# Self-attention of one core: six small moves in an order of work written out by hand

## The chip, the cores and the metric

One core of a Trainium2 chip runs the kernel. Times are device microseconds (us). The median of three runs before the change is 2024.88 us (2024.06 to 2028.83).

## The reference, cut to what matters

The input is x with 2 batches of 512 rows of 512 channels. Three blocks follow each other, each added to x:

```
x = x + cross_attention(layernorm(x), ctx)   # 8192 context rows, 16 heads
x = x + attention(layernorm(x))              # causal, 16 heads of 32
x = x + experts(layernorm(x))                # 16 experts, top 2
```

The self-attention, which the change touches, computes per head

```
q_amp, k_amp = softplus(x Wq_amp), softplus(x Wk_amp), each over its root mean square
q_phi, k_phi = pi * tanh(x Wq_phi), pi * tanh(x Wk_phi)
scores = q_amp cos(q_phi) . k_amp cos(k_phi) + q_amp sin(q_phi) . k_amp sin(k_phi)
out = softmax(scaled, causal scores) (x Wv) Wo
```

## The kernel before

The cross-attention fills the first 1550 us or so, the self-attention lies between 1572 and 1875 us, and the experts come after it. The change is in the self-attention alone.

The 1024 rows are eight tiles of 128. A tile t goes through two strands. The strand `ahead` makes its queries, keys and values: normalise (`xn`), transpose on TensorE (`turn`), copy out (`copy`, and `low` for the f16 remainder), the five projections (`p01`, `p23`, `p4`), the softplus (`abs`, `exp`, `ln`, and `relu` on ScalarE for tiles 2 and later, then `amp` on VectorE adds the two), `square`, `mean`, `mroot`, `norm` for the root mean square, `phase` (a table load, tanh, two sines and a table load back, all on ScalarE; the second sine waits for `tabs` on VectorE), `polar` (amplitude times sine and cosine, in two halves 0 and 1), and `qkT`/`qkC` (transposes and copies of queries and keys). The other strand attends: for each pair of heads p (64 pairs over the 8 tiles) `scoreT` on TensorE, `expT` on ScalarE, for two pairs together `cut` (mask and key sums) and then `valueT` on TensorE and `normT` on VectorE. `woT` is the output projection of a tile, `x3` adds it to x, `rT`, `rC`, `router`, `logit` and so on prepare the expert stage.

Round a of 8 pairs (pairs 8a to 8a+7) attends with tile a and prepares tile a+1; it has 16 slots, two per pair. `slot(a, k)` calls `ahead(a+1, k)`, then the steps for tile a-1 from a table (`carry`: slot number to steps), then the others. A pair p issues: `scoreT`, slot 2(p mod 8), `expT`, for odd pairs `normT` and `cut`, slot 2(p mod 8)+1, for even pairs `valueT`. `self_order` lists all of this once, and each engine runs through the same list and executes its own kinds in that order, strictly one after another. Nothing is reordered at run time, so a wait of one instruction holds all behind it on its engine.

Banks of the matmul accumulator are handed on by `empty(banks, semaphore, value)` and `fill(banks)`: the step that fills a bank waits for the semaphore that `empty` noted last. Banks 0 and 1 hold the `p01` result, which `abs`, `relu` (tiles 2 and later) or `amp` (tiles 0 and 1) read; `turn` and `router`/`colsum`/`cum` fill them next. Bank 3 is filled by `woT` after `phase` has read it.

Tiles 2 and later use f16 weights in two parts, a high part (`high`, two ScalarE copies per weight, line 1433) and the remainder (`rest`, two VectorE operations per weight, line 1774). Weights 0 and 1 are split before round 0, weights 2, 3 and 4 in round 0. `p23` of tile 2 (round 1, slots 0 and 2) needs the parts of weights 2 and 3, `p4` of tile 2 (round 1, slot 6) those of weight 4.

Lines: 1107 `turn`; 1121 and 1126 `p01`, `p23`, `p4` in f32 and f16; 1135 `qkT`; 1165 `scoreT`; 1180, 1184 and 1188 `valueT`; 1195 `woT`; 1497 `expT`; 1362 table load; 1761 `xn`; 1770 `amp`; 1784 `square`; 1788 and 1791 `mean`; 1802 `tabs`; 1808 `polar`; 1816 `qkC` of the keys; 1845 to 1856 `cut`; 1862 and 1866 `normT`; 1875 `x3`; 1890 `logit`; 1244 and 1250 `colsum` and `router`. `stats 1` (lines 1824, 1367, 1369, 1603 to 1609) makes the scale factors of rows 512 and up by a Newton step, and stands ahead of `expT 8`.

Of the kernel before, what the change touches and what calls it, by code (L numbers as in the profile page):

```python
# [23 lines left out]
HALVES = 2  # L24
# [366 lines left out]
def self_order(kept):  # L391
# [5 lines left out]
    out, emptied = [], {}  # L397

    def fill(banks):
        return tuple(emptied[b] for b in banks if b in emptied)  # L400

    def empty(banks, name, value):
        for b in banks:
            emptied[b] = (name, value)

    def p23(t, n):
        out.append(("p23", t, n, fill((2 + n // 2,)) if n % 2 == 0 else ()))

    def p01(t, n):
        out.append(("p01", t, n, fill((n // 2,)) if n % 2 == 0 else ()))  # L410

    def p4(t, n):
        out.append(("p4", t, n, fill((1,)) if n == 0 else ()))

    def turn(t):
        out.append(("turn", t, fill((0,))))
        empty((0,), "xTs", t + 1)

    def qkT(t, w, half):
        out.append(("qkT", t, w, half, fill((2 + half,))))  # L420
        empty((2 + half,), ("QT", "KT")[w], 2 * t + half + 1)

    up = (10, 11, 12, 14)

    def ahead(t, slot, begun=False):
        if slot < 4 and not begun:
            p23(t, slot)
        if slot < 3:
            out.append((("abs", "exp", "ln")[slot], t))
        if slot == (3 if begun else 2) and t >= HALVES:  # L430
            out.append(("relu", t))
        if slot == 3:
            out.append(("amp", t))
            empty((0, 1), "amp", t + 1)
            if t < 7:
                out.append(("xn", t + 1))
        elif slot == 4:
            out.append(("square", t))
            if t < 7:
                turn(t + 1)  # L440
        elif slot == 5:
            out.append(("phase", t))
            empty((2, 3), "phi", t + 1)
            out.append(("mean", t))
        elif slot == 6:
            out.append(("tabs", t))
            p4(t, 0)
        elif slot == 7:
            if t < 7:
                out.append(("copy", t + 1))  # L450
                if t + 1 >= HALVES:
                    out.append(("low", t + 1))
            out.append(("mroot", t))
            p4(t, 1)
            empty((1,), "sv", t + 1)
        elif slot == 8:
            out.append(("vcopy", t))
            out.append(("norm", t))
        elif slot == 9:
            out.append(("polar", t, 0))  # L460
        elif slot == 10:
            qkT(t, 0, 0)
            out.append(("polar", t, 1))
        elif slot == 11:
            out.append(("qkC", t, 0, 0))
            qkT(t, 0, 1)
        elif slot == 12:
            out.append(("qkC", t, 0, 1))
            qkT(t, 1, 0)
        elif slot == 13:  # L470
            out.append(("qkC", t, 1, 0))
            qkT(t, 1, 1)
        elif slot == 14:
            out.append(("qkC", t, 1, 1))
        if t < 7 and slot in up:
            p01(t + 1, up.index(slot))

    def follow(f, step):
        if step == "wo0" or step == "wo1":
            n = int(step[2])  # L480
            out.append(("wo" if kept else "woT", f, 2 * n, 2 * n + 2, fill((3,)) if n == 0 else ()))
            empty((3,), "x3", f + 1)
        elif step == "rT":
            bank = 2 if f < 6 else 3
            out.append(("rT", f, bank, fill((bank,))))
            empty((bank,), "rC", f + 1)
        elif step == "rC":
            out.append(("rC", f, 2 if f < 6 else 3))
        elif step == "router":
            bank = 1 if f < 5 else 3  # L490
            out.append(("router", f, bank, fill((bank,))))
            empty((bank,), "lg", f + 2)
        elif step == "logit":
            out.append(("logit", f, 1 if f < 5 else 3))
        else:
            out.append((step, f))

    carry = {8: ["wo0"], 9: ["wo1"], 10: ["x3"], 11: ["stat"], 12: ["lroot"], 13: ["lnr", "xn3"], 14: ["rT"], 15: ["rC"]}
    late = {4: ["wo0"], 5: ["wo1"], 6: ["x3", "stat"], 7: ["lroot"], 8: ["lnr", "xn3"], 9: ["rT"], 10: ["rC"],
            11: ["router"], 13: ["logit"]}  # L500
    if not kept:
        late = {4: ["wo0"], 5: ["wo1"], 6: ["x3", "stat"], 7: ["lroot"], 8: ["lnr", "xn3"], 10: ["rT"], 11: ["rC"],
                13: ["router"], 14: ["logit"]}

    halving = {6: ("high", 2), 8: ("rest", 2), 9: ("high", 3), 11: ("rest", 3), 13: ("high", 4), 15: ("rest", 4)}

    def slot(a, k):

        if a < 7:
            ahead(a + 1, k)  # L510
        if 1 <= a < 8:
            for step in (carry if a < 7 else late).get(k, ()):
                follow(a - 1, step)
        if a == 6 and k == 4:
            out.append(("cum", 0, 1, fill((1,))))
        if a == 1 and k == 4:
            out.append(("colsum", 0, fill((1,))))
            empty((1,), "lg", 1)
        if a == 1 and k == 5:
            out.append(("negsum", 0))  # L520
        if a == 0 and k in halving:
            out.append(halving[k])
        if 2 <= a < 8 and k == (4 if a < 7 else 1):
            follow(a - 2, "router")
        if 2 <= a < 8 and k == (5 if a < 7 else 2):
            follow(a - 2, "logit")
        if a == 5 and k in (6, 8, 9, 11, 13):
            out.append((("rank", "odds", "first", "second", "shares")[(6, 8, 9, 11, 13).index(k)], 0))
        if a == 6 and k == 5:
            out.append(("place", 0, 1))  # L530
            empty((1,), "cumr", 1)
        if a == 6 and k == 7:
            out.append(("rows", 0))
# [6 lines left out]
    for k in range(3):  # L540
        ahead(0, k)
    p23(0, 3)
    begun, out = out, []
# [3 lines left out]
    for k in range(3, 16):  # L547
        ahead(0, k, k == 3)
        for pieces in (wide, sums, halved):
            if k in pieces:  # L550
                out.append(pieces[k])
    if kept:
        for p in range(67):
            a, k = p // 8, 2 * (p % 8)
# [31 lines left out]
    else:  # L586
        for p in range(64):
            a, k = p // 8, 2 * (p % 8)
# [58 lines left out]
def build(nc, A, out):  # L647
    ctx = ExitStack()
    with ctx:
# [123 lines left out]
        s6.close()  # L773

        begun, order = self_order(False)
        kept = self_order(True)[1]
        first = {what: [ev for ev in begun if ev[0] == what] for what in ("turn", "p01", "p23")}

# [1304 lines left out]
```

## Time and profile before

| | |
|---|---|
| median of 3 runs | 2024.88 us |
| profiled execution, its own time | 2023.89 us |
| its span | 2022.1 us |
| TensorE matmul (PE) busy | 1893.6 us, 94% |
| VectorE (DVE) busy | 1706.4 us, 84% |
| ScalarE (ACT) busy | 1468.8 us, 73% |

The span is what the trace covers, and the profiled execution's own time is 1.8 us more. Busy shares over the whole span are mostly those of the cross-attention. In the rows below, a row of a timeline gives start, duration, engine, line, operation, output and input, and in square brackets the idle time just before and who ended it. "x8" says that eight instructions are taken together. A row of the chain of waits gives start, duration, engine, output, line. A row of the table by stretches gives the stretch, its length, then busy time and instruction count of PE, PEld (TensorE weight loads), DVE, ACT and POOL, then the granted TensorE clock (1.00 is 2.4 GHz, 0.50 is 1.2 GHz), the DMA share and GB/s.

### The profile page before, as it was taken

To read this page: it belongs to the slowest core of one execution; us is meant where nothing else is said; L and a number is where in the kernel's file an instruction comes from. 1 tells how busy PE (TensorE), PEld (TensorE's weight loads), DVE (VectorE), ACT (ScalarE), POOL (GpSimd) and SP (SyncE) were. 2 spreads that over 40 slices of the span, in tenths; PEclk is the share of its full clock that TensorE was granted. 3 is DMA by queue.
4 is the path that set the end of the run, shared out by engine and by line. 5 is a ranking of instruction groups with operands and counts; after the bars stand their busy time and mean duration, and the time that the engine had idled before them with its cause. 6 is when DMAs were issued, how large, how long until landed. Compare 5 with 4: busy or idle time off the path is not lost.

```text
span 2022.1 us, 31194 instructions
## 1 busy us (share of the span) xinstructions
PE 1893.6 (94%) x11838; PEld 780.0 (39%) x11838; DVE 1706.4 (84%) x1500; ACT 1468.8 (73%) x1671; POOL 46.3 (2%) x57
## 2 busy tenths in 40 slices
PE   7899999999999999989999999999999989998593
PEld 3333333333333333333333333333332445555582
DVE  5699999999999999788999999999996587886354
ACT  2488888888888888768888888888886545553120
POOL 2000000000000000000000000000000000001103
PEclk9999999999999999999999999999999979999797
DMA  7433322333333224222323333333240000007574
GB/s 246 167 102 91 99 79 79 89 92 92 85 93 99 79 78 120 79 78 73 85 79 85 93 86 92 89 87 97 63 137 32 23 1 1 1 1 261 208 260 146
DMA packets 113354, 194.58 MB, mean 96 GB/s; under 512 B 10288, under 2 KB 64560, under 8 KB 113200
## 3 DMA queue, kind: packets, MB, share of 16 engines
q1 hardware_dynamic: 110640, 184.12, 30.8%
q0 software_dynamic: 2560, 8.39, 1.3%
q8 instruction: 99, 1.62, 0.3%
q14 instruction: 55, 0.45, 0.1%
HBM read 109.63 MB, written 50.33 MB: 79 GB/s over the span
## 4 chain that ended last, share of the span: by engine, by line
PE 83%; DVE 7%; issue 3%; ACT 3%; DMA 2%; POOL 1%; SPq 1%; POOLq 0%; ACTq 0%; DVEq 0%
PE ps L1088 22%; PE ps L1275 22%; PE ps L1002 12%; PE ps L1005 11%; PE ps L1334 3%; PE ps L1126 2%; DVE dacc L1705 2%; PE ps L1165 1%; PE ps L1121 1%; PE ps L1028 1%; PE ps L1075 1%; PE ps L1344 1%; PE ps L1195 1%; PE ps L1135 1%; POOL og L978 1%
## 5 line engine op out<-in xcount | busy, mean ns | idle before, releaser
L1537 ACT ACTIVATE pt<-ps,bias 128x1024 f32<-128x1024 f32 x1024 | 1110.0, 1114 | 216.7 <-PE ps L1275 216.4
L1705 DVE TENSOR_TENSOR dacc<-dacc,pt 128x2048 f32<-128x2048 f32 x496 | 1135.1, 2288 | 58.7 <-ACT pt L1537 34.5
L1275 PE MATMUL ps<-qst,kst 128*128 128x512 f16 x2048 | 613.0, 382 | 15.8 <-ACT pt L1537 15.0
L1088 PE MATMUL ps<-pt,vt 128*32 128x512 f32 x4096 | 493.6, 598 | 0.0
L1275 PEld LDWEIGHTS ps<-qst,kst 128*128 128x128 f16 x2048 | 178.2, 98 | 421.9 <-ACT pt L1537 125.6
L1002 PE MATMUL ps<-wsm 128*128 128x512 f16 x1152 | 314.6, 384 | 14.7 <-DVE wsm L1663 10.8
L1005 PE MATMUL ps<-wsm 128*128 128x512 f16 x1152 | 310.4, 380 | 5.2 <-ACT vt L1389 2.9
L1088 PEld LDWEIGHTS ps<-pt,vt 128*32 128x32 f32 x4096 | 106.8, 109 | 263.1 <-issue 241.5
L1002 PEld LDWEIGHTS ps<-wsm 128*128 128x128 f16 x1152 | 113.4, 99 | 157.0 <-DVE wsm L1663 10.8
L1005 PEld LDWEIGHTS ps<-wsm 128*128 128x128 f16 x1152 | 112.5, 98 | 143.9 <-ACT vt L1389 3.8
L1648 DVE SCALAR_TENSOR_TENSOR wsm<-ps,wsm 128x512 f16<-128x512 f32 x128 | 88.0, 687 | 30.0 <-ACT wsm L1385 29.8
L1497 ACT ACTIVATE pT<-ps 128x256 f32<-128x256 f32 (+3 forms) x64 | 44.5, 702 | 66.9 <-PE ps L1165 66.7
L1385 ACT ACTIVATE wsm<-ps 128x512 f16<-128x512 f32 x128 | 75.8, 592 | 16.6 <-PE ps L1002 12.9
L1716 DVE TENSOR_TENSOR oacc<-ps,oacc 128x512 f32<-128x512 f32 x120 | 82.2, 685 | 5.7 <-PE ps L1088 3.4
L1389 ACT ACTIVATE vt<-ps 128x512 f32<-128x512 f32 x128 | 76.2, 596 | 3.1 <-PE ps L1005 3.1
L1165 PE MATMUL ps<-QT,KT 64*128 64x128 f32 x640 | 53.3, 295 | 12.4 <-ACT pT L1497 12.4
L1988 DVE SCALAR_TENSOR_TENSOR wsm<-wsm 128x512 f16<-128x512 f32 x90 | 61.5, 683 | 0.0
L972 POOL DMA_INDIRECT xbuf<-xn,diu x16 | 17.1, 1066 | 1840.3 <-DVE diu L1960 1836.0
L2032 DVE TENSOR_SCALAR sg<-sg 128x256 f32<-128x256 f32 x16 | 4.7, 294 | 61.0 <-ACT sg L1578 61.0
L1545 ACT ACTIVATE wsm<-wsm 128x512 f16<-128x512 f32 x90 | 55.9, 621 | 0.0
L1165 PEld LDWEIGHTS ps<-QT,KT 64*128 64x128 f32 x640 | 41.5, 190 | 31.4 <-issue 31.4
L1126 PE MATMUL ps<-wsm,xT 128*128 128x512 f16 x216 | 51.5, 390 | 1.0 <-DVE lg L1890 0.6
(203 smaller groups left out, 1193.2 us busy)
## 6 DMA issues: line engine op xcount, KB each, us to landing
kst<-kscr SPq DMA_DIRECT2D x132, 256.0 KB, 3.5
kscr<-wsm SPq DMA_DIRECT2D x128, 256.0 KB, 3.5
kst<-kst SPq DMA_DIRECT2D x124, 256.0 KB, 3.4
wsm<-in_ctx SPq DMA_DIRECT2D x32, 768.0 KB, 4.8
qst<-qscr SPq DMA_DIRECT2D x32, 128.0 KB, 2.9
xbuf<-xn SPq DMA_DIRECT2D x16, 256.0 KB, 6.2
wsm<-in_gate SPq DMA_DIRECT2D x8, 512.0 KB, 5.1
wsm<-in_fc SPq DMA_DIRECT2D x8, 512.0 KB, 6.0
```

Of the source, the lines that this page charges most:

```text
L1002: p = e.matmul(ps[:, at, :], wk[:, wi, c, u * 128:u * 128 + 128], chl[:, j, ci_, c, :], start=n == 0, stop=n == 8)
L1005: p = e.matmul(ps[:, at, :], chl[:, j, ci_, c, u * 128 - 512:u * 128 - 384], wv[:, wi, c, :], start=n == 0, stop=n == 8)
L1088: p = e.matmul(ps[32 * h:32 * h + 32, 4 + n % 2, :], vt[:, kb % 2, ch, c:c + 32], pt[:, (2 * i + h // 2) % 6, h % 2, :], start=ch == 0, st ...
L1126: p = e.matmul(ps[:, b0 + n, :], xhl[:, t % 2, xi, c * 128:c * 128 + 128], whl[w0 + n][:, wi, c, :], start=m == 0, stop=m == 11)
L1165: m = e.matmul(ps[:, bk + h, 128 * k:128 * k + 128], KT[64 * h:64 * h + 64, hp, c:c + 128], QT[64 * h:64 * h + 64, t % 3, hp, :], start=Tr ...
L1275: p = e.matmul(ps[:, 2 * half + h2, :], kst[:, kb % 2, h, ch * 128:ch * 128 + 128], qst[:, h, :], start=True, stop=True)
L1385: e.activation(khl[:, u % 2, 0], ps[:, at, :], ACT.Copy, scale=KS / (WS * CS)).then_inc(S["khi"], 1)
L1389: e.activation(vt[:, j, u - 4, :], ps[:, at, :], ACT.Copy, scale=1.0 / (WS * CS)).then_inc(S["vev"], 1)
L1537: e.activation(pt[:, (2 * i + half) % 6], ps[:, 2 * half:2 * half + 2, :], ACT.Exp, bias=bias[:, 4 * kb + ch:4 * kb + ch + 1], scale=SCORE ...
L1648: e.scalar_tensor_tensor(out=khl[:, u % 2, 1], in0=ps[:, at, :], scalar=KS / (WS * CS), in1=khl[:, u % 2, 0], op0=ALU.mult, op1=ALU.subtra ...
L1705: e.tensor_tensor(own_heads, own_heads, probs, ALU.add).then_inc(S["add"], 1)
L1716: e.tensor_tensor(oacc[:, g, :], ps[:, 4 + n % 2, :], oacc[:, g, :], ALU.add).then_inc(S["oac"], 1)
```

## The change

Seen per step, it does this:

- `relu` of tiles 2 and later goes from slot 2 (in `ahead`, after `ln`) to slot 1 (ahead of `exp`), and banks 0 and 1 are noted as empty from there, by `relu`, and no longer from `amp` in slot 3. For tiles 0 and 1 nothing changes in this.
- `xn` of the next tile goes from slot 3 (behind `amp`) to slot 1, for t of 1 and more; for t = 0 it stays in slot 3 and stands ahead of `amp`.
- `woT` of the tile before goes from slots 8 and 9 to slots 6 and 7, in rounds 1 to 6. `x3` and what follows it stay.
- `high` and `rest` of weights 2, 3 and 4 go from slots 6, 8, 9, 11, 13, 15 of round 0 to slots 11 to 15 of round 0 and slot 1 of round 1.

```diff
     def ahead(t, slot, begun=False):
         if slot < 4 and not begun:
             p23(t, slot)
+        if slot == 1 and t >= HALVES:
+            out.append(("relu", t))
+            empty((0, 1), "relu", t - HALVES + 1)
         if slot < 3:
             out.append((("abs", "exp", "ln")[slot], t))
-        if slot == (3 if begun else 2) and t >= HALVES:
-            out.append(("relu", t))
+        if slot == (1 if t else 3) and t < 7:
+            out.append(("xn", t + 1))
         if slot == 3:
             out.append(("amp", t))
-            empty((0, 1), "amp", t + 1)
-            if t < 7:
-                out.append(("xn", t + 1))
+            if t < HALVES:
+                empty((0, 1), "amp", t + 1)
...
-    carry = {8: ["wo0"], 9: ["wo1"], 10: ["x3"], 11: ["stat"], 12: ["lroot"], 13: ["lnr", "xn3"], 14: ["rT"], 15: ["rC"]}
+    carry = {6: ["wo0"], 7: ["wo1"], 10: ["x3"], 11: ["stat"], 12: ["lroot"], 13: ["lnr", "xn3"], 14: ["rT"], 15: ["rC"]}
...
-    halving = {6: ("high", 2), 8: ("rest", 2), 9: ("high", 3), 11: ("rest", 3), 13: ("high", 4), 15: ("rest", 4)}
+    halving = {(0, 11): ("high", 2), (0, 12): ("rest", 2), (0, 13): ("high", 3), (0, 14): ("rest", 3),
+               (0, 15): ("high", 4), (1, 1): ("rest", 4)}
...
-        if a == 0 and k in halving:
-            out.append(halving[k])
+        if (a, k) in halving:
+            out.append(halving[a, k])
```

## Rows read from the trace of the kernel before

**Rows 1.** Table by stretches; first two in rounds 0 and 1, then rounds 2 and 6.

```profile
1623.00:1626.00 3.00, 0.25 (x2) 0.28 (x3) 2.93 (x5) 0.00 (x0) 0.00 (x0) 0.50 0.00 0
1650.00:1652.00 2.00, 2.00 (x21) 1.13 (x11) 1.97 (x3) 0.95 (x1) 0.00 (x0) 0.50 0.00 0
...
1671.00:1705.00 34.00, 31.41 (x317) 19.41 (x315) 26.10 (x47) 19.16 (x26) 0.00 (x0) 1.00 0.01 2
1805.00:1840.00 35.00, 29.64 (x358) 19.63 (x358) 29.56 (x58) 19.89 (x27) 9.38 (x8) 1.00 0.52 184
```

**Rows 2.** Chain of waits, round 0.

```profile
1614.01 1.28 ACT L1362
1615.30 2.00 ACT wsm L1433 x2
1617.60 0.69 DVE pT L1850
...
1621.17 2.36 DVE wsm L1774 x2
...
1624.38 1.24 DVE qc L1808
1625.75 1.09 PE ps L1135 x4
...
1634.92 0.69 DVE KT L1816
1635.61 0.88 DVE pr L1862
```

**Rows 3.** Timeline, rounds 0 and 1.

```profile
1617.71 0.80 PE L1165 MATMUL ps<-QT,KT 64*128 64x128 f32 x4 [3.72 <-ACT pT L1497]
1626.63 2.77 PE L1126 MATMUL ps<-wsp,xT 128*128 128x512 f16 x6
1635.81 1.47 PE L1126 MATMUL ps<-wsp,xT 128*128 128x512 f16 x6
1640.27 0.16 DVE L1603 TENSOR_TENSOR rt<-rs 128x4 f32<-128x4 f32 x1 [0.51 <-ACT rs L1369]
1645.52 1.22 DVE L1770 TENSOR_TENSOR amp<-amp,t 128x1024 f32<-128x1024 f32 x1
1646.66 0.54 DVE L1761 TENSOR_SCALAR xn<-xs,mv,rs 128x512 f32<-128x512 f32 x1
1647.11 1.22 DVE L1784 TENSOR_TENSOR t<-amp 128x1024 f32<-128x1024 f32 x1
1647.34 0.63 PE L1107 MATMUL ps<-ident,xn 128*128 128x128 f32 x4 [2.16 <-DVE xn L1761]
1651.54 4.56 PE L1126 MATMUL ps<-wsm,xT 128*128 128x512 f16 x12
1658.43 2.36 DVE L1808 TENSOR_TENSOR qc<-qc,amp 128x1024 f32<-128x1024 f32 x2
1661.74 0.66 PE L1135 MATMUL ps<-ident,qc 128*128 128x128 f32 x4
```

**Rows 4.** Timeline, round 3.

```profile
1710.88 0.96 DVE L1862 RECIPROCAL pr<-ps 128x128 f32<-128x128 f32 x1 [3.79 <-PE ps L1184]
1717.50 0.63 PE L1107 MATMUL ps<-ident,xn 128*128 128x128 f32 x4 [1.80 <-DVE xn L1761]
1721.18 2.76 PE L1126 MATMUL ps<-wsm,xT 128*128 128x512 f16 x12
1725.22 1.16 PE L1165 MATMUL ps<-QT,KT 64*128 64x128 f32 x16 [1.28 <-ACT pT L1497]
1726.31 3.70 PE L1195 MATMUL ps<-wo,aT 128*128 128x512 f32 x8
1730.73 2.36 DVE L1808 TENSOR_TENSOR qc<-qc,amp 128x1024 f32<-128x1024 f32 x2
1732.27 0.65 PE L1135 MATMUL ps<-ident,qc 128*128 128x128 f32 x4
```

## The prediction

> **What bounds the kernel now.** I read the table by stretches first, then the chain of waits over the self-attention, then the timeline of single rounds. By stretches, TensorE is idle for 2.6 of the 34 us of round 2 and for 5.4 of the 35 us of round 6 [rows 1]: a round is paced by TensorE most of the time, with a few holes, and in a hole another engine sets the end. The chain of waits names them. In round 0 it runs through a table load, then the two ScalarE copies of `high 2` (2.00 us), then a `cut`, then the two VectorE operations of `rest 2` (2.36 us), then `polar`, and only then TensorE goes on with `qkT` at 1625.75 [rows 2]. So the splitting of the weights stands on the path that sets the end. The timeline has the hole at the front of it, 3.72 us ahead of `scoreT 4` [rows 3]. In the later rounds there are two holes, ahead of `turn` (1.80 us in round 3, for `xn`) and ahead of the first `scoreT` behind `phase` (1.28 us) [rows 4]. In round 1 the first of these is 2.16 us [rows 3]. The granted clock is 0.50, the 1.2 GHz level, at 1623 to 1626 and at 1650 to 1652, each time behind such a hole, and 1.00, the 2.4 GHz level, over rounds 2 and 6, holes included [rows 1].
>
> **The change, part one: the splitting in round 0.** `high 2` leaves the place between the table load and `expT 3`. The load ends at 1615.29, so `expT 3` starts there and not 2.00 us later (1.9 on VectorE, whose `cut` follows it at 1617.60). `rest 2` leaves the place ahead of `polar 1 0`, 2.3 us more. `polar` then starts at 1624.38 - 1.9 - 2.3 = 1620.2 and `qkT 1 0 0` at 1621.6, 4.2 us sooner than now [rows 2]. `high 3`, which now sits behind `expT 4`, goes too, and holds nothing there any more.
>
> What is given back stands behind it. All six pieces now come between `qkT 1 0 0` and round 1. On ScalarE each `high` (2.00) lies beside projections of tile 2 on TensorE, and I cost them at nothing: between two `expT` TensorE has `qkT` and six matmuls or more. If that cover were gone they would cost up to 2 us each. On VectorE `rest 2` lies ahead of the key copies as `rest 3` did, which is no change. But `rest 3` now stands ahead of `normT 2` and `cut 3`, and `rest 4` ahead of `normT 3`, `cut 4` and `amp 2`. From `qkT` to the start of the last key copy stays 9.2 us (1625.75 to 1634.92 [rows 2]), if the clock there is as now. The VectorE queue is then: copies done at 1621.6 + 9.2 + 0.6 = 1631.4, `rest 3` 2.36, `normT 2` and `cut 3` 1.9 (0.88 and 0.3 for the two parts of `normT`, 0.69 for `cut`), `stats 1` 1.5 (five operations of about 0.16 and a trip over ScalarE that shows as 0.51 [rows 3]), `xn 3` 0.54, `rest 4` 2.36, `normT 3` and a `cut 4` of two operations 2.6. That puts `amp 2` at 1642.7, where it is now at 1645.52 [rows 3]. Part one is worth 2.9 us at `amp 2`; 1.3 of the 4.2 us go back to VectorE. Bounds: 0 if VectorE and the `expT 8` behind `stats 1` take all back, 5.0 if the clock stays at 2.4 GHz, since then TensorE does the stretch sooner: six matmuls of `p01` take 2.77 us there and 1.47 at the full clock [rows 3], and with the transposes that is up to 2.9 us, of which VectorE's queue lets 2.1 through. I take the low clock: TensorE would still have holes of 1.8 and 3.6 us there, against 3.72 and 5.5 now.
>
> **Part two: `relu`, the banks and `xn`.** `relu` trades places with `exp` and `ln`; all three end before the next `expT` either way, so ScalarE's sum is the same and this alone costs nothing. `xn` of 0.54 us leaves the place between `amp` and `square`, where it holds the latter by 0.45 us (1646.66 to 1647.11 [rows 3]). In slot 1 VectorE is idle: 3.79 us ahead of `normT 11` in round 3 [rows 4]. `turn` and `router` no longer wait for `amp` and `xn`; TensorE moves on by 1.80 us in round 3, but `p4` behind them waits for `logit`, which comes only 0.45 us sooner, behind `square` and `mean`. So most of that hole moves to `p4`, as 0.6 us, or is closed by the shift. What counts is the VectorE chain `amp`, `square`, `mean`, `tabs`, second sine, table load, `expT`, `cut`, `norm`, `polar`: 0.45 us sooner per round. In round 0 `turn 2` and `amp 1` still hang together; in the step for t = 0 `xn` and `amp` swap, and `turn 1` then waits for `amp` in place of `xn`: nothing. In round 6 there is no `xn` to move: nothing.
>
> **Part three: `woT` two slots sooner.** Its eight records (3.70 us [rows 4]) now stand between `scoreT` and `valueT` behind the hole of 1.28 us. They go ahead of that `scoreT`, beside `phase`. From the start of `p4` TensorE then has in round 3: 2.7 for `p4`, 3.6 for `woT`, two `scoreT` of 1.1 and a `valueT` of 1.25, 9.8 us in all, from about 1720.0 to 1729.8. `polar 4 0`, which `qkT` waits for, ends now at 1730.73 + 1.23 = 1731.96 [rows 4] and then at 1731.5, so the queue is done 1.7 us ahead of it. `scoreT 28` itself comes later than now, by about 1.2 us, and only because there is slack does this cost nothing; with no slack it would cost just that. `qkT` now starts 0.31 us behind the end of `polar`; the least that I see is 0.13 us (1625.62 to 1625.75 [rows 2]). A round thus gains 0.45 from part two and the rest here: 0.45 + 0.31 - 0.13 = 0.63 us in round 3. The same rows in rounds 2, 4 and 5 give 0.69, 0.69 and 0.63, the last held to 0.45 by a wait for `x3`. Sum over rounds 2 to 5: 2.5 us, bounds -1.0 (each `scoreT` delay on the path, less the gain) and 5 (the whole of the hole ahead of `turn` less what `p4` keeps). From `qkT` to the next `amp` TensorE is nearly full, so the shift goes through.
>
> In round 1 the same sum is larger. `polar 2 0` ends at 1659.66 and `qkT 2 0 0` starts at 1661.74 [rows 3], 2.08 us behind it, because `p4` took 4.56 us at the 1.2 GHz level where 12 such matmuls take 2.76 in round 3 [rows 3, 4], and `woT` followed. Without that queue: 0.45 + 2.08 - 0.13 = 2.4 us. This holds if the clock stays up. If it falls, `p4` and `woT` take some 3 us more against a slack of 1.2, and 1.2 to 1.8 of the 2.4 are lost.
>
> One rule speaks against a part of this. The Trainium skill, "TensorE: Matmul & The Clock Gate", section "A second HAM failure mode: psum-queue depth-cycling", says that an engine which idles briefly and often between groups of matmuls, as it cycles through its accumulator banks, can swing between the two clock levels, so that its bursts lose throughput. By that rule each round could fall to 1.2 GHz, and the sum would lose about what the fourth case below loses. The rows of rounds 2 and 6 stand at 1.00 with such holes in them, so this trace does not agree for holes of this size.
>
> Round 6 and the tail: `woT 5` comes sooner, but `qkT 7 0 0` waits for `polar` there and VectorE's chain has no `xn`; 0.1 us, cost at nothing. SP's expert loads wait for the last `p4`, which now ends 1.8 us later in its round; they have over 40 us before the first expert, so nothing.
>
> **Sum.** 2.9 + 2.4 + 2.5 = 7.8 us. On the profiled execution 2023.89 - 7.8 = 2016.1; the median of the runs is 0.99 us above that execution, so 2017.1 us.
>
> **The rivals.** First, the clock holds at 2.4 GHz in round 0 as well: 5.0 + 2.4 + 2.5 = 9.9, 2015.0 us. For it, the holes get shorter; against it, 3.6 us of hole are left, and a hole of 2.16 was enough in round 1. Second, the clock falls again in round 1, since TensorE there waits some 2 us for `negsum` ahead of `p4`: 2.9 + 1.0 + 2.5 = 6.4, 2018.5 us. For it speaks the fall now at 2.16 us. Third, the change does less than it says: `rest 3`, `rest 4` and the `expT 8` behind `stats 1` take all of part one back, and `woT` ahead of `scoreT` delays `expT` and `valueT` so that rounds 2 to 5 gain nothing. Then round 1's 2.4 is left, with up to 2 us more or less: 2022.5 us. For it speaks that VectorE is busy 26.10 of 34 us in round 2 [rows 1]; against it its hole ahead of `normT`. Fourth, slower: with `woT` gone from behind `scoreT`, TensorE has its longest hole (1.5 us) ahead of `qkT`, behind one of 0.6 us, and the clock falls there in each of rounds 2 to 5. Then `qkT` and the projections behind it run at 1.2 GHz as they do now in round 0, at 2.9 us a round: 4 x 2.9 = 11.6 against 7.8, so 3.8 us slower, 2028.7 us. It decides against the change from three rounds on. Against it: the holes of a round sum to 3.1 us now and to about 2.3 then, and the clock is at 1.00 now. The same page, section "HAM oscillation — how this bites in real kernels", describes a kernel that pays such a fall at every wait; here it shows in rounds 0 and 1 alone.
>
> **Chances.** Forecast 0.40 (its own range 2015.6 to 2018.7), first rival 0.15, second 0.15, third 0.23, fourth 0.07. What a measurement can tell from no change is 0.3%, 6.1 us, so faster begins at 2018.8. The forecast, the first rival and two thirds of the second lie below it: 0.37 + 0.15 + 0.10 = 0.62. The third and the remainders are the same, 0.31, and slower is 0.07. The range from 2014.4 to 2022.6 takes in the first two rivals and half of the third, and leaves out about 0.2.
>
> **What would show it.** Right: `high 2` off the chain and `scoreT 4` about 1.8 us behind `p4` and not 3.72; `qkT 1 0 0` some 4.2 us sooner against the start of round 0; `rest 3` and `rest 4` on the chain ahead of `amp 2`; no wait of `turn` for `xn`, and a small one of `p4` for `logit`; `qkT` of rounds 1 to 5 starting 0.13 us behind `polar`; the clock at 1.00 around round 1's `p4`. Wrong: `qkT` held by TensorE's own queue, a clock of 0.50 in rounds 2 to 5, or an `amp 2` as late as now.

## The result, and the profile after

The median of nine runs is 2020.39 us (2018.06 to 2022.97), that of nine runs of the kernel before beside them 2027.03 us (2024.06 to 2028.83). The ratio is 0.9969 [0.9961, 0.9977]: 6.3 us less, 4.7 to 7.9. The forecast was 2017.1 us and 7.8 us less. Of the 3.3 us between the two times 2.1 come from the starting point: the three runs that the forecast went by had their median at 2024.88. The other 1.2 are the gain, since the two medians lie 6.6 us apart. By the ratio the gain came 1.5 us smaller than forecast, and 7.8 still lies inside its interval.

The profiled execution took 2022.89 us by its own time (span 2021.1), among the longest of the nine. The work ahead of `scoreT 0`, nearly all of it the unchanged cross-attention, took 2.82 us more in it: `scoreT 0`, the first step of round 0, begins at 1603.00, before at 1600.18. So everything below is read as a distance from `scoreT 0`. In that measure the end of the span comes 3.82 us sooner (421.92 before, 418.10 after).

All lines stand 3 further down: 1107 is now 1110, 1808 is 1811. The table by stretches, the same stretches as in [rows 1] moved with the work, and one of 4 us near the end of round 6:

```profile
1623.00:1626.00 3.00, 1.59 (x6) 1.15 (x7) 2.96 (x4) 0.47 (x1) 0.00 (x0) 0.50 0.00 0
1650.00:1652.00 2.00, 2.00 (x7) 0.96 (x6) 1.40 (x3) 1.71 (x2) 0.00 (x0) 1.00 0.00 0
1669.00:1702.00 33.00, 30.87 (x312) 19.18 (x313) 25.67 (x47) 19.35 (x26) 0.00 (x0) 1.00 0.01 1
1802.00:1837.00 35.00, 30.93 (x357) 21.04 (x357) 29.57 (x58) 19.87 (x27) 9.37 (x8) 0.95 0.47 169
1827.00:1831.00 4.00, 2.98 (x21) 2.48 (x21) 3.93 (x7) 1.19 (x2) 3.39 (x3) 0.68 1.03 367
```

In round 0 the clock still falls to 0.50, the 1.2 GHz level. In round 1 it is 1.00 now where it was 0.50. Round 6, which stood at 1.00, has 0.95 over it, because of a fall near its end that the last row shows. The chain of waits in round 0, against [rows 2]:

```profile
1616.82 1.28 ACT L1365
...
1618.53 0.69 DVE pT L1853
...
1623.04 1.24 DVE qc L1811
...
1634.50 2.27 DVE wsm L1777 x2
...
1640.38 2.27 DVE wsm L1777 x2
...
1645.08 1.23 DVE amp L1773
1646.34 1.24 DVE t L1787
```

`high` and `rest` are gone from between the table load and `polar`. `polar 1 0` begins 20.04 us behind `scoreT 0`, before 24.20. `rest 3` and `rest 4` (the two rows of `wsm`) now stand on the chain ahead of `amp 2`. The timeline of rounds 0 and 1, against [rows 3]:

```profile
1618.64 0.49 PE L1168 MATMUL ps<-QT,KT 64*128 64x128 f32 x4 [1.83 <-ACT pT L1500]
1624.41 1.09 PE L1138 MATMUL ps<-ident,qc 128*128 128x128 f32 x4 [3.35 <-DVE qc L1811]
1625.29 2.77 PE L1129 MATMUL ps<-wsp,xT 128*128 128x512 f16 x6
1644.01 0.66 PE L1110 MATMUL ps<-ident,xn 128*128 128x128 f32 x4
1649.17 1.47 PE L1129 MATMUL ps<-wsm,xT 128*128 128x512 f16 x6 [2.27 <-DVE negs L1897]
1657.65 2.36 DVE L1811 TENSOR_TENSOR qc<-qc,amp 128x1024 f32<-128x1024 f32 x2
1659.02 0.63 PE L1138 MATMUL ps<-ident,qc 128*128 128x128 f32 x4 [1.51 <-DVE qc L1811]
```

The hole ahead of `scoreT 4` went from 3.72 to 1.83 us. `turn` begins before `amp` (1645.08) and waits for nothing. The wait moved to `p4`, 2.27 us for `negsum`, and its six matmuls still take 1.47 us. In round 3, against [rows 4]:

```profile
1716.80 1.47 PE L1129 MATMUL ps<-wsm,xT 128*128 128x512 f16 x6 [0.75 <-DVE lg L1893]
...
1727.04 2.36 DVE L1811 TENSOR_TENSOR qc<-qc,amp 128x1024 f32<-128x1024 f32 x2
1728.41 0.63 PE L1138 MATMUL ps<-ident,qc 128*128 128x128 f32 x4 [1.79 <-DVE qc L1811]
```

The two holes of 1.80 and 1.28 us are now 0.75 us ahead of `p4` and 1.79 us ahead of `qkT`. `qkT` starts 0.14 us behind the end of the first `polar` (1727.04 + 1.23). The gain by stretches, for this execution, for another of the same kernel (e0) and for a kernel that is told of below (e9), in us against the profiled execution of before. The profiled executions of e0 and e9 are the fastest of their kernels' runs, so the columns do not compare typical runs:

| stretch | forecast | changed | e0, changed again | e9, with fillers |
|---|---|---|---|---|
| at `qkT 1` | 4.2 | 4.16 | 4.17 | 3.47 |
| at `amp 2` | 2.9 | 3.26 | 4.79 | 5.57 |
| `amp 2` to `qkT 2` | 2.4 | 2.28 | 2.17 | 2.28 |
| `qkT 2` to `qkT 6` | 2.5 | 0.42 | 2.08 | 2.10 |
| `qkT 6` to `qkT 7` | 0 | -0.16 | -0.16 | -0.17 |
| `qkT 7` to the end of the self-attention | 0 | -1.04 | -1.03 | 0.01 |
| expert stage | 0 | -0.94 | 0.01 | 0.13 |
| sum, without the row at `qkT 1` | 7.8 | 3.82 | 7.86 | 9.92 |

### The profile page after: what moved, and what is told of

It reads as the page before. It is cut to its first block, busy times and chain, and to the rows that moved or that the text cites. A ratio compares the mean times of both kernels' runs of the same rounds, so it can differ in the third digit from the quotient of the medians.

```text
span 2021.1 us, 31193 instructions
## 1 busy us (share of the span) xinstructions
PE 1894.2 (94%) x11838; PEld 782.0 (39%) x11838; DVE 1706.8 (84%) x1500; ACT 1468.4 (73%) x1671; POOL 46.6 (2%) x57
## 4 chain that ended last, share of the span: by engine, by line
PE 83%; DVE 8%; issue 3%; ACT 2%; DMA 2%; POOL 1%; SPq 1%; POOLq 0%; DVEq 0%; ACTq 0%
PE ps L1091 22%; PE ps L1278 22%; PE ps L1005 12%; PE ps L1008 11%; PE ps L1337 3%; PE ps L1129 2%; DVE dacc L1708 2%; PE ps L1124 1%; PE ps L1031 1%; PE ps L1078 1%; PE ps L1347 1%; PE ps L1168 1%; PE ps L1138 1%; POOL og L981 1%; ACT pt L1540 1%
```

## The experiments

**The changed kernel again (e0), and its parts alone.** e0_again has no edit. Each of the next three is the kernel before with one part of the change.

> The changed kernel once more, for a second profile and more times. In the profile of the changed kernel the clock fell to 0.50 at 1760 to 1763 in round 4 and at 1867, which cost about 1.6 us at qkT 6 and about 1 us in the tail. Theory A (these falls come and go from execution to execution): the distances from scoreT 0 to qkT 1, amp 2, qkT 2 to qkT 5 come back within 0.3 us (21.4, 42.1, 56.0, 89.1, 125.4, 156.7), and the ones behind a fall differ by 1 us or more, with the fall at another place or absent. Rival B (the new order makes the fall in round 4): qkT 6 again at 188.8 with a clock of 0.50 around qkT 5. Time: 6 us (0.3%) below the kernel before.

Measured: 2020.19 us, ratio 0.9964 [0.9952, 0.9976], 7.3 us less. The executions of one kernel differ where the clock is low. In e0 it is low in round 0 and around `p4` of round 1, but not in rounds 2 to 5, and these give 2.08 us. `amp 2` had been expected at 42.1 us and came at 40.55, since the clock of round 0 came back sooner. The execution above has one fall there, at 1760 to 1763, and gives 0.42. The fall in round 4 is thus not a matter of the order alone; one near the end of round 6 (1824) and one in the tail (1861) came in both.

e1_halving:

```diff
-    halving = {6: ("high", 2), 8: ("rest", 2), 9: ("high", 3), 11: ("rest", 3), 13: ("high", 4), 15: ("rest", 4)}
+    halving = {(0, 11): ("high", 2), (0, 12): ("rest", 2), (0, 13): ("high", 3), (0, 14): ("rest", 3),
+               (0, 15): ("high", 4), (1, 1): ("rest", 4)}
```

> Only the six splitting steps are moved, the rest is the kernel before. Theory A (part one stands by itself): qkT 1 at 21.4 us from scoreT 0 in place of 25.6, amp 2 at 42.1 to 42.5 in place of 45.3; from amp 2 on as in the kernel before, so that 2.9 to 3.3 us are left at the end, 0.15% of the time. Rival B (the gain shows only with the other parts): amp 2 at 45, and under 1 us at the end. It also shows what relu after ln does with the high copies ahead of abs: up to 1 us later at amp 2 than in the changed kernel if that place matters.

Measured: 2022.8 us, 0.9978 [0.9969, 0.9988], 4.5 us. `qkT 1` comes 4.16 us sooner and `amp 2` 5.23 sooner. So part one carries some 60 to 70% of the gain (4.5 of the 7.3 and 6.3 us of the two measurements of the whole change, with an interval of 2.4 to 6.3). That is more than the 2.9 to 3.3 us expected. `amp 2` comes 0.44 us sooner than in e0, with the clock low for as long; in e1 `xn 3` (0.54 us) still stands behind it. In rounds 2 to 5 this kernel is laid out as before, and yet the interval from `qkT 3` to `qkT 4` grew from 36.85 to 37.06 us, where the clock fell. Its table by stretches, the 4 us ahead of the fall and those of the fall:

```profile
1712.00:1716.00 4.00, 2.20 (x24) 1.52 (x22) 3.93 (x6) 2.15 (x2) 0.00 (x0) 1.00 0.00 0
1716.00:1720.00 4.00, 4.00 (x56) 3.46 (x56) 3.90 (x7) 2.56 (x4) 0.00 (x0) 0.61 0.00 0
```

TensorE stood for 1.80 of 4 us and fell behind that. The same hole of 1.80 us stands in the kernel before [rows 4], and the clock stayed at 1.00. A second fall, at 1816 in round 6, came with no hole over 0.54 us in the 20 us ahead of it, and cost nothing there: `qkT 6` to `qkT 7` takes 34.39 us, before 34.40.

e2_strand (`relu`, the banks and `xn`) and e3_wot (`woT`):

```diff
# e2_strand
+        if slot == 1 and t >= HALVES:
+            out.append(("relu", t))
+            empty((0, 1), "relu", t - HALVES + 1)
...
+        if slot == (1 if t else 3) and t < 7:
+            out.append(("xn", t + 1))
# e3_wot
-    carry = {8: ["wo0"], 9: ["wo1"], 10: ["x3"], ...
+    carry = {6: ["wo0"], 7: ["wo1"], 10: ["x3"], ...
```

> Only relu, the release of banks 0 and 1, and xn are moved. Theory A (the VectorE chain sets the end): every round from 1 to 5 gains 0.45 us, because xn is off the chain; woT stays in the queue ahead of qkT and moves with it. Sum 2.2 us at qkT 6, plus up to 1.8 us in round 1 if the clock no longer falls there. Rival B (the hole ahead of turn is what costs): 1 to 1.8 us per round, 6 us in all. Rival C (all of it is hidden): under 0.1 us per round.

> Only woT is moved two slots ahead. Theory A (it takes away only the few tenths that qkT starts behind polar): 0.15 to 0.25 us per round in rounds 2 to 5, 0.8 us in all; in round 1, where p4 runs at 0.50, between 0.8 us lost and 0 gained, unless the clock stays up. Rival B (it fills the hole ahead of scoreT, so it is worth its 1.3 to 1.5 us per round): 5 us or more. Rival C (scoreT and expT come later and hold the round): 0.5 to 1.2 us lost per round.

Measured: e2 2026.07 us, 0.9995 [0.9986, 1.0004]; e3 2026.44 us, 0.9995 [0.9986, 1.0004]. Alone, neither can be told from no change. The trace says why. Where no clock falls, the round from `qkT 2` to `qkT 3` takes 33.68 us before, 33.35 in e2, 33.46 in e3 and 33.1 with both: 0.33 and 0.22 add up to the 0.55 to 0.6 of the whole. From `amp 2` to `qkT 2` they save 2.1 and 1.8 us of 16.22, which does not add up: both together save 2.3. In both the clock was also low for a shorter time there (not at all in e2, 1651 to 1655 in e3, against 1648 to 1655 before), so how round 1's gain divides between the moves and the clock is not shown. For e3 this was a miss, as 0 to 0.8 us lost had been expected unless the clock stays up. Against these savings stands in e2 a fall at 1725 (`qkT 3` to `qkT 4` takes 38.19 us, where e5 below, with the same `xn` in that stretch, takes 36.52), 1.7 us, and in both an early fall in the tail, told of below, 1.05 and 0.8 us. At the end of their traces e2 is 0.5 us ahead and e3 1.0. The timeline of e3 in round 1, lines as before:

```profile
1650.15 0.63 PE L1107 MATMUL ps<-ident,xn 128*128 128x128 f32 x4 [2.16 <-DVE xn L1761]
1654.22 1.70 PE L1126 MATMUL ps<-wsm,xT 128*128 128x512 f16 x6
1655.76 1.88 PE L1195 MATMUL ps<-wo,aT 128*128 128x512 f32 x4
```

`turn` has the old hole of 2.16 us, and `woT` stands ahead of the `scoreT` behind `phase`: what it no longer holds is `qkT 2`.

**The strand taken apart, and a second look at before.** e5_xn moves `xn` alone, e6_banks `relu` and the banks alone, b0_again has no edit.

```diff
# e6_banks
+        if slot == 1 and t >= HALVES:
+            out.append(("relu", t))
+            empty((0, 1), "relu", t - HALVES + 1)
# e5_xn
+        if slot == (1 if t else 3) and t < 7:
+            out.append(("xn", t + 1))
```

> The kernel before once more, for a second profile. Theory A (falls of the clock come and go from execution to execution there too): the distances between qkT 2 and qkT 5 that no fall touches come back within 0.1 us (33.7, 36.9, 31.8), and the clock falls at some place in rounds 2 to 6, where the first profile had none; round 0 has its long stretch at 0.50 again. Rival B (only the new order has falls behind round 1): no clock under 0.95 between 1660 and 1860.

> Only relu goes to slot 1 and releases banks 0 and 1; xn stays behind amp. Theory A (the VectorE chain sets the end, so the banks alone give nothing): distances between qkT 2 and qkT 6 as before, 33.7, 36.9, 31.8 and 30.9, within 0.05 us where the clock holds, since turn still waits for xn. Rival B (the banks carry the gain): 0.3 us or more off each, as with relu, banks and xn together (33.35, 31.57, 30.59).

> Only xn is moved to slot 1, banks 0 and 1 are still released by amp. Theory A (VectorE's chain loses 0.45 us a round, and that is all that the strand's part gives): distances between qkT 2 and qkT 6 of 33.35, 36.5, 31.57 and 30.6 where the clock holds, the same as with relu, banks and xn together. Rival B (xn alone gives nothing, since turn then waits for amp and p4 for router and logit as before): 33.7, 36.9, 31.8, 30.9.

Measured, one run each: b0 2024.8, e6 2024.98, e5 2023.5 us. b0's distances lie within 0.2 us of those of before, up to the end of the self-attention. It has no fall of the clock between 1660 and 1860, where the first theory had expected one: the second trace of before is as steady there as the first. The round from `qkT 2` to `qkT 3` takes 33.68 us in e6, as before, and 33.35 in e5, as in e2. So `xn` carries all of part two in these rounds, and the banks nothing. (`amp 2` comes 1.3 us sooner in e6 than before, where the clock was low for some 10 us of round 0 and not some 14.) The timeline of round 2, e6 first (lines 2 further down), then e5:

```profile
1682.15 0.63 PE L1109 MATMUL ps<-ident,xn 128*128 128x128 f32 x4 [1.08 <-DVE xn L1763]
```

```profile
1679.24 1.22 DVE L1770 TENSOR_TENSOR amp<-amp,t 128x1024 f32<-128x1024 f32 x1
1680.50 1.23 DVE L1784 TENSOR_TENSOR t<-amp 128x1024 f32<-128x1024 f32 x1
1680.52 0.66 PE L1107 MATMUL ps<-ident,xn 128*128 128x128 f32 x4 [0.54 <-DVE amp L1770]
```

In e6 the banks are free, and `turn` waits for `xn` behind `amp`. In e5 it waits for `amp`, but `square` stands right behind `amp` (1679.24 + 1.22 to 1680.50), and the time follows from that.

**The clock, by filling the holes.** The changed kernel with matmuls of a constant into a free bank, which nothing reads. e7_spin0 has them in round 0 (in slot 7 for 12 matmuls, in slot 10 ahead of `qkT 1` for 32), e8_spinall has 12 more ahead of `qkT 2` to `qkT 6`.

```diff
+            if SPIN.get(t):
+                out.append(("spin", t, SPIN[t], fill((2,))))
             qkT(t, 0, 0)
...
+                elif what == "spin":
+                    for k in range(4 * ev[2]):
+                        c = slice(128 * (k % 4), 128 * (k % 4) + 128)
+                        e.matmul(ps[:, 2, c], ident[:], ones[:], start=True, stop=True)
```

> The changed kernel with idle time of TensorE in round 0 filled: 12 matmuls of 128 columns (1.3 us) ahead of scoreT 4 and 32 (about 3.4 us) ahead of qkT 1, into a bank that nobody reads before it is overwritten. They compute nothing that is used. Theory A (the low clock is the price that part one still pays): the clock stays at 1.00 over round 0, amp 2 comes at 40.0 to 40.5 us from scoreT 0 in every execution, where it was 42.1 and 40.6 in two executions of the changed kernel, and the time falls by 0.5 to 2 us against the changed kernel. Rival B (the filler holds the queue): qkT 1 later than 21.4, up to 22.5, and amp 2 at 41 or more. Rival C (the clock falls all the same): amp 2 at 42 to 44, since the filler then takes twice its time.

> As the one before, and 12 more such matmuls (1.3 us) ahead of qkT 2 to qkT 6, where TensorE waits 1.4 to 1.8 us for polar. Theory A (falls of the clock in rounds 2 to 5 cost 1.3 to 1.7 us each and come in about one round of an execution): no clock under 0.95 between round 1 and round 5, distances between qkT 2 and qkT 6 at 33.1, 36.3, 31.3 and 30.4 us, none of them 1.2 us longer, and a time 1 to 3 us below the changed kernel. Rival B (the filler delays qkT): each distance 0.1 to 0.5 us longer, time unchanged or slower. Rival C: the falls come as before.

Measured: e7 2023.7 us, 0.9982 [0.9973, 0.9991]; e8 2027.54 us, 1.0 [0.9991, 1.0009]. As tests of time both missed. I had the fillers half as long as they are, and in e7 the clock fell in rounds 1 and 3 all the same, which took 1.3 and 1.7 us more. The timeline of e7, then that of e8:

```profile
1616.91 2.84 PE L1150 MATMUL ps<-ones,ident 128*128 128x128 f32 x24
1621.17 7.41 PE L1150 MATMUL ps<-ones,ident 128*128 128x128 f32 x64
...
1628.85 1.46 PE L1136 MATMUL ps<-wsp,xT 128*128 128x512 f16 x6
...
1650.18 2.74 PE L1136 MATMUL ps<-wsm,xT 128*128 128x512 f16 x6 [2.27 <-DVE negs L1908]
```

```profile
1657.78 2.94 PE L1150 MATMUL ps<-ones,ident 128*128 128x128 f32 x24
```

Each f32 matmul of 128 columns is two records of 0.116 us, and 32 of them held `qkT 1` by 3.7 us. Of the clock they tell something, e7 first: it stays at 1.00 over round 0 (six matmuls 1.46 us, not 2.77), and from `qkT 1` to `amp 2` pass 17.67 us, against 20.67 in the changed kernel and 19.15 in e0. In round 1, which has no filler in e7, it falls at 1649, `p4` takes 2.74 us and not 1.47, and from `amp 2` to `qkT 2` pass 15.19 us, against 13.94 in the changed kernel. In e8 the one fall left in rounds 0 to 6 lies at 1832, but 2.94 us of filler do not fit into holes of 1.8, and its rounds from `qkT 2` to `qkT 6` come 0.9 to 1.3 us longer than those of the changed kernel where no clock falls.

e9_fill cuts them to the holes: 5 matmuls in slot 7 and 12 ahead of `qkT 1`, 5 ahead of `qkT 2` to `qkT 6`, 7 ahead of `qkT 7`, and 8 ahead of `p4` of tile 2. The edit against e8:

```diff
-SPIN = {1: 8, 2: 3, 3: 3, 4: 3, 5: 3, 6: 3}
+SPIN = {1: 12, 2: 5, 3: 5, 4: 5, 5: 5, 6: 5, 7: 7}
...
-                    for k in range(4 * ev[2]):
+                    for k in range(ev[2]):
```

> The fillers again, cut to the holes. Each f32 matmul of 128 columns took 0.23 us (two records of 0.116), twice what the last two kernels with fillers were laid out for, so those held qkT by 3.7 us in round 0 and about 1.1 us a round later. Now 5 (1.2 us) ahead of scoreT 4, 12 (2.8 us) ahead of qkT 1, 8 (1.9 us) ahead of the first p4 of round 1, 5 ahead of qkT 2 to 6 and 7 (1.6 us) ahead of qkT 7. They compute nothing that is used. Theory A (the low clock is what the changed kernel still pays, about 2 us in round 0 and 1.2 to 1.7 us at each later fall): no clock under 0.95 up to 1850, qkT 1 at 21.4 to 21.6, amp 2 at 39.5 to 40.2, distances of 33.1, 36.3, 31.3, 30.4, 34.6 and then 48.4, and 2 to 4 us off the changed kernel's time. Rival B (the fillers cost as much as they save, by tenths of a us at each place): distances 0.1 to 0.4 longer, time as the changed kernel or slower.

Measured: 2016.74 us (2015.77 to 2019.27), 0.9949 [0.9935, 0.9962], 10.3 us less than before and the best of all kernels here. Its interval just touches that of the changed kernel and overlaps e0's at 0.9952 to 0.9962; its median lies 3.5 us below theirs, and four of its five runs lie below all fifteen of theirs. Its timeline of round 0, and its table by stretches:

```profile
1615.65 1.28 PE L1152 MATMUL ps<-ones,ident 128*128 128x128 f32 x10
1617.64 0.49 PE L1181 MATMUL ps<-QT,KT 64*128 64x128 f32 x4 [0.72 <-ACT pT L1513]
1619.69 4.57 PE L1152 MATMUL ps<-ones,ident 128*128 128x128 f32 x24
...
1624.53 1.46 PE L1138 MATMUL ps<-wsp,xT 128*128 128x512 f16 x6
```

```profile
1621.00:1624.00 3.00, 3.00 (x18) 3.00 (x18) 2.90 (x5) 0.00 (x0) 0.00 (x0) 0.58 0.00 0
1624.00:1626.00 2.00, 2.00 (x15) 1.32 (x14) 1.97 (x4) 1.27 (x2) 0.00 (x0) 1.00 0.00 0
...
1801.00:1836.00 35.00, 31.19 (x414) 22.92 (x416) 29.22 (x58) 18.26 (x25) 9.37 (x8) 1.00 0.60 213
```

The fillers met the fall in their own time (24 records take 4.57 us, not 2.8) and cost `qkT 1` 0.7 us, but the clock is back when `qkT` and the projections begin, and from there to the expert stage it does not fall again.

**A tighter order of the splitting.** e10_order puts `rest` in the slot of its `high`; e11_both is e9 with this order.

```diff
-    halving = {(0, 11): ("high", 2), (0, 12): ("rest", 2), (0, 13): ("high", 3), (0, 14): ("rest", 3),
-               (0, 15): ("high", 4), (1, 1): ("rest", 4)}
+    halving = {(0, 11): (("high", 2), ("rest", 2)), (0, 12): (("high", 3), ("rest", 3)), (0, 13): (("high", 4),),
+               (1, 1): (("rest", 4),)}
```

> The changed kernel with the splitting one place tighter: high 2 and rest 2 in slot 11, high 3 and rest 3 in slot 12, high 4 in slot 13 of round 0, rest 4 in slot 1 of round 1. rest 3 then lies in VectorE's idle time ahead of the key copies and not ahead of normT 2 and cut 3, and high 4 no longer stands ahead of abs 2. Theory A (VectorE's and ScalarE's queues between qkT 1 and amp 2 give back part of the 4.2 us): amp 2 comes 0.8 to 1.2 us sooner than in the changed kernel at the same clock, that is 41.0 where the clock is low as in its first profile and 39.5 where it recovers early. Rival B (TensorE alone sets amp 2, by its clock): no difference beyond the clock's. Rival C: the key copies come late and hold scoreT 8: amp 2 later.

> Both of the two before together: fillers cut to the holes, and the tighter splitting. If both theories hold, amp 2 at 38.5 to 39.3 us from scoreT 0, no fall of the clock until round 7, and the lowest time of all, 3 to 5 us below the changed kernel. If the clock alone is what amp 2 hangs on, the same as with the fillers alone.

Measured: e10 2019.88 us, 0.9963 [0.995, 0.9977]; e11 2018.0 us (2016.46 to 2020.36), 0.9956 [0.9942, 0.9969]. The timeline of e10:

```profile
1628.53 2.36 DVE L1777 SCALAR_TENSOR_TENSOR wsm<-wsm 128x1024 f16<-128x1024 f32 x2 [0.46 <-ACT wsm L1436]
...
1641.34 1.22 DVE L1773 TENSOR_TENSOR amp<-amp,t 128x1024 f32<-128x1024 f32 x1
```

`amp 2` comes 39.74 us behind `scoreT 0`, 0.8 sooner than in e0, but the times of e10 and e0 are the same within their intervals, and e11 adds nothing to e9. e11 had been expected to be the fastest of all, with no fall before round 7. Its `amp 2` comes at 39.50 us, 0.27 sooner than in e9, but the clock fell at 1828 in round 6 in spite of the fillers, and `logit` behind it came 1.1 us later. So fillers of this size do not rule a fall out.

## Why the prediction was right, and where it was not

**Part one, 2.9 us at `amp 2`.** The mechanism held to the tenth: `qkT 1` 4.16 us sooner (4.2 foretold), `scoreT 4` 1.83 us behind its predecessor (about 1.8), `rest 3` and `rest 4` on the chain. Its size is off, and always to the good side: 3.26, 4.79 (e0) and 5.23 (e1), the last over my upper bound of 5.0, as is e9's 5.57. I had taken the clock as low as before. How long it stays low is what differs: in slices of 1 us it stands below 1.00 for some 11 us in the changed kernel's trace (1620 to 1631), and for some 8 in those of e0 (1618 to 1626) and e1 (1621 to 1629). The cover for the `high` pieces on ScalarE held, since the bound of 5.0 was reached, and the 2.1 us that I had VectorE's queue let through at the full clock were too few.

**Round 1, 2.4 us.** 2.28 in the changed kernel, at a clock of 1.00 around `p4`, and 2.17 in e0, where the stretch 1644 to 1651 has a clock of 0.76. I had `p4` and `woT` at the low clock eat 1.2 to 1.8 us of the term (the second rival). So short a dip did not. The dip of e7, twice as long, took 1.25 of the 2.28 us: there the second rival's condition and its price both came.

**Rounds 2 to 5, 2.5 us.** Where the clock holds, they give 2.08 us in e0: 0.56, 0.54, 0.44 and 0.54 in rounds 2 to 5, where 0.69, 0.63, 0.69 and 0.45 were foretold. The steps are as told: `turn` waits for nothing, `p4` 0.75 us for `logit`, `qkT` starts 0.14 us behind `polar`. The split is measured: `xn` 0.33 and `woT` 0.22 in round 2, where I had 0.45 and about 0.2.

**What was missing from the sum.** The step "Round 6 and the tail ..., cost at nothing" failed in two ways. First, the move of `woT` costs 0.16 us between `qkT 6` and `qkT 7`: e3 has it too (34.56 us against 34.40), e5 and e6 don't. The second half of `qkT 6` waits for `x3`, 0.50 us in the changed kernel's timeline and in e3's:

```profile
1794.23 0.66 PE L1138 MATMUL ps<-ident,qc 128*128 128x128 f32 x4 [0.50 <-DVE xs L1878]
```

Second, the 1.04 us of the tail (1.03 in e0). They arise some 40 us behind `qkT 7`, at the transposes of tile 7 for the expert stage and its `router`, which `logit` waits for. These ran at 0.50, since the clock fell at 1866, where in the kernel before it fell at 1874, behind them. The changed kernel first, then before:

```profile
1865.95 1.07 PE L1242 MATMUL ps<-ident,xs 128*128 128x128 f32 x4 [0.87 <-DVE xs L1878]
1867.75 1.86 PE L1253 MATMUL ps<-wr,aR 128*128 128x16 f32 x8 [0.73 <-ACT aR L1526]
...
1868.93 0.63 PE L1239 MATMUL ps<-ident,xs 128*128 128x128 f32 x4 [0.88 <-DVE xs L1875]
1870.29 1.04 PE L1250 MATMUL ps<-wr,aR 128*128 128x16 f32 x8 [0.73 <-ACT aR L1523]
```

```profile
1866.00:1870.00 4.00, 2.88 (x12) 2.40 (x12) 2.04 (x10) 0.89 (x3) 0.00 (x0) 0.50 0.00 0
...
1869.00:1873.00 4.00, 1.59 (x12) 1.28 (x12) 2.90 (x13) 1.15 (x4) 0.00 (x0) 1.00 0.00 0
```

Eight of the fourteen traces have this early fall in the tail and pay 0.8 to 1.1 us for it. Among them are e1 and e6, which keep `woT` in its old place; before, b0, e5, e9 and e11 do not have it, and in e7 it came in between, for 0.3 us. Whether the change makes it likelier is not shown.

Besides these, single falls of the clock came in the rounds where the kernel before had none: at 1760 (1.66 us, 2.08 less 0.42) and at 1828 in the changed kernel, at 1824 in e0. The one near the end of round 6 cost nothing: the next `logit` comes 12.13 us behind `qkT 7` in the changed kernel and before alike. The places, first in the changed kernel's timeline, then in its table by stretches:

```profile
1759.72 0.69 PE L1138 MATMUL ps<-ident,qc 128*128 128x128 f32 x4 [1.38 <-DVE qc L1811]
1760.20 2.77 PE L1129 MATMUL ps<-wsp,xT 128*128 128x512 f16 x6
...
1826.37 0.63 PE L1138 MATMUL ps<-ident,qc 128*128 128x128 f32 x4 [2.22 <-DVE qc L1811]
```

```profile
1760.00:1762.00 2.00, 2.00 (x9) 0.87 (x8) 2.00 (x3) 0.60 (x1) 0.00 (x0) 0.54 0.00 0
```

And in round 3 of e10, where the hole of 1.8 us is the same as the changed kernel's, which did not fall there:

```profile
1724.68 0.64 PE L1138 MATMUL ps<-ident,qc 128*128 128x128 f32 x4 [1.80 <-DVE qc L1811]
```

```profile
1726.00:1728.00 2.00, 2.00 (x7) 0.96 (x6) 1.97 (x5) 0.00 (x0) 0.00 (x0) 0.50 0.00 0
```

All of these falls came within 2.1 us behind the hole ahead of `qkT`. That is the fourth rival's mechanism, in the place where it was put: the change turned a hole of 1.80 us ahead of `turn` and one of 1.28 ahead of `scoreT` into 0.75 and 1.79 us, the longer one now ahead of `qkT`, and in round 6 one of 2.22 ahead of `qkT 7`, where the longest had been 1.38. Falls behind `turn`'s hole came as well, at 1716 to 1723 in e1, e3, e5 and e6, but they cost 0 to 0.3 us: the projections there have slack up to `polar`. Behind `qkT`'s hole (the changed kernel, e7, e10) and behind one of 1.97 us ahead of `scoreT` in e2 a fall cost 1.7, for TensorE is nearly full from `qkT` to the next `amp`. So my price of 2.9 us was 1.2 us too high, and so was the count: none or one in rounds 2 to 5, not four. The five traces with `xn` in its old place (before, b0, e1, e3, e6) have none of these falls of 1.7 us in rounds 2 to 5, four of the six with it moved and without fillers there (the changed kernel, e2, e7, e10; not e0, e5) have one. That is in favour of a link with the order, but eleven traces do not prove one, and e1 has a fall without a long hole. In round 6 the 2.22 us come from moving `woT` (1.84 in e3, where it moves alone); both traces of the changed kernel fell behind it, at no cost.

A fall of 1.7 us in some of the executions and the 1.0 us of the tail are of the size of the 1.5 us by which the gain fell short of 7.8. For the median this is inferred, since the other executions have no trace, and the interval of the ratio allows no shortfall at all. That e0's trace comes out at 7.86 us is in part luck: part one gave 1.9 us more than its term, and rounds 1 to 5 gave 0.65 less, and the move of `woT` (0.16) and the tail (1.03) were not in the sum. Why one hole of 1.8 us brings a fall and the next does not stays open. The Trainium skill, "TensorE: Matmul & The Clock Gate", section "A second HAM failure mode: psum-queue depth-cycling", says that short idle times between groups of matmuls can make the clock swing. I held against it that rounds 2 and 6 stood at 1.00 over their holes. The new traces agree with the page halfway: no swing from group to group, but one fall to 0.50 in a round now and then.

**The first rival** (the clock holds in round 0, 9.9 us, 2015.0) was not the changed kernel, but it is very nearly e9: 9.92 us in its trace, 10.3 in its median. Its term of 5.0 for `amp 2` was 5.57, though the fillers hold `qkT 1` by 0.7. **The third rival** (VectorE takes part one back, 2022.5) is refuted by `amp 2` in every trace with part one in it: it comes 2.5 us sooner or more, even behind the long fillers of e7 and e8.

## What to carry to other kernels

- When the splitting of weights, or any preparation that nothing needs yet, stands in the queues of two engines ahead of a chain that the third waits for, move it behind that chain: here it was 4.5 us of the 6.3 to 7.3. What it lands on has to be followed up to the first step that both queues meet at.
- Freeing a buffer sooner is worth something only if the data that fill it are there sooner as well (e6 nothing, e5 the whole of that part), and what shortened the round was not the freed wait but the 0.5 us operation taken out of VectorE's chain.
- Where TensorE is near full, ask which work stands right behind its longest holes: a fall of the clock there was nearly free ahead of work with slack and cost 1.7 us ahead of work that sets the time. A few matmuls of a constant, cut to the hole by their measured duration, bought another 3.5 us in e9 (1.9 in e11 against e10, within the intervals); cut too long they cost all of the gain.

## What the runs showed of the hardware

- A fall of the clock behind a hole of 1.4 to 1.8 us is a matter of the execution: the same instructions in the same order showed it at 1760 in one profiled run, behind 1.38 us, and not in another, behind 1.37 us.
- The f32 matmul of 128 columns shows as two records of 0.116 us at the full clock, 0.23 us in all, and as two of 0.19 us where the clock was low for most of them (24 records in 4.57 us in e9).
- The expert stage, untouched, took 0.94 us more in the changed kernel's trace than in e0's, and the work ahead of `scoreT 0` 2.82 us more than in the trace of before. Differences of this size between two profiled executions say nothing of the change, and only a reading stretch by stretch keeps them out of it.
